# One core, post-norm decoder layer: the last batch's transposed self scores directly behind its self scores, and the work of the last steps placed anew

## The reference, cut to what matters

```
x = layernorm(x + self_attention(x))        # causal; rms norm and rope on q and k
x = layernorm(x + cross_attention(x, ctx))  # causal; q from x, k and v from ctx
x = layernorm(x + light_ffn(x) + heavy_ffn(x))
```

## Time and profile before

| what | value |
|---|---|
| median of three runs | 978.58 us (974.46 to 981.06) |
| the profiled execution, its own time | 978.16 us |
| its span, first to last instruction | 976.4 us |
| what lies around the span | 1.76 us |
| mean granted PE clock | 0.96 |
| busy, share of the span | PE 91%, PEld 71%, DVE 74%, ACT 51%, POOL 55% |
| DMA queue of SP | 50.5% of 16 engines |

### The profile page before, as it was taken

The page is one execution under the profiler, slowest core; times in us unless marked ns, Lnnn a source line. Parts: engine busy times, 40 slices in busy tenths (PEclk is TensorE's granted clock), DMA queues, the critical chain, the costliest instruction groups (busy, mean ns, idle before and its releaser), DMA issues. The chain is left out here.

```text
span 976.4 us, 21698 instructions
## 1 busy us (share of the span) xinstructions
PE 888.3 (91%) x7712; PEld 689.7 (71%) x7712; DVE 725.3 (74%) x1764; ACT 496.8 (51%) x1063; POOL 537.9 (55%) x1047
## 2 busy tenths in 40 slices
PE   3367897999999999999999999999999999999886
PEld 2335565787868787777878787877778686767576
DVE  7788687878788878879787888788887877663411
ACT  1132444646475655656464756556464746455332
POOL 7554465646564756656565647657565656162421
PEclk9669898999999999999999999999999999999888
DMA  3794383727476654818275666738283656613000
GB/s 110 120 173 68 52 110 50 106 33 109 51 100 78 98 78 65 111 37 110 34 119 59 100 78 80 97 54 107 44 109 42 95 72 88 77 31 49 14 11 21
DMA packets 79644, 74.22 MB, mean 76 GB/s; under 512 B 8593, under 2 KB 78897, under 8 KB 79537
## 3 DMA queue, kind: packets, MB, share of 16 engines
q1 hardware_dynamic: 75008, 68.11, 50.5%
q10 hardware_dynamic: 4528, 4.73, 1.9%
HBM read 17.49 MB, written 4.20 MB: 22 GB/s over the span
## 5 line engine op out<-in xcount | busy, mean ns | idle before, releaser
L768 ACT ACTIVATE pr<-bank 128x384 f32<-128x384 f32 x512 | 240.0, 500 | 188.1 <-PE bank L370 187.0
L946 DVE TENSOR_REDUCE mx<-bank 128x3 f32<-128x384 f32 x512 | 266.4, 552 | 89.7 <-PE bank L370 87.5
L1311 POOL TENSOR_SCALAR_AFFINE_SELECT pr<-pr 128x256 f32<-128x256 f32 x512 | 222.1, 448 | 132.3 <-ACT pr L768 130.1
L370 PE MATMUL bank<-w,g 128*128 128x256 f32 x576 | 170.8, 389 | 1.1 <-ACT g L780 1.1
L370 PE MATMUL bank<-cmaskb,idb 128*128 128x256 bf16 x512 | 143.3, 280 | 27.7 <-DMA stk2k<-nat1k 13.7
L780 ACT ACTIVATE g<-bank,b 128x256 f32<-128x256 f32 x144 | 67.8, 473 | 83.5 <-PE bank L370 83.2
L1335 POOL TENSOR_TENSOR xTlow<-xT,xThigh 128x512 fp32r<-128x512 f32 x16 | 20.8, 1301 | 149.8 <-ACT xThigh L702 149.8
L370 PEld LDWEIGHTS bank<-w,g 128*128 128x128 f32 x576 | 89.6, 190 | 5.2 <-ACT g L780 1.5
L370 PEld LDWEIGHTS bank<-cmaskb,idb 128*128 128x128 bf16 x512 | 50.1, 98 | 50.5 <-DVE mx L946 22.5
L370 PE MATMUL bank<-stk2k,stk2q 97*128 97x128 bf16 (+1 forms) x512 | 85.1, 253 | 0.0
L370 PE MATMUL bank<-stk1q,stk1k 100*128 100x256 bf16 (+1 forms) x512 | 80.1, 254 | 2.4 <-DMA stk1q<-mT 1.0
(11 more groups left out here) (166 smaller groups left out, 1832.5 us busy)
## 6 DMA issues: line engine op xcount, KB each, us to landing
stk1q<-nat1q SPq DMA_DIRECT2D x90, 128.0 KB, 4.5
stk1k<-nat1k SPq DMA_DIRECT2D x90, 128.0 KB, 5.4
stk2k<-nat2k SPq DMA_DIRECT2D x90, 128.0 KB, 4.6
stk2q<-nat2q SPq DMA_DIRECT2D x90, 128.0 KB, 5.7
xT<-in_xT SPq DMA_DIRECT2D x16, 256.0 KB, 5.9
ctxT<-in_ctxT SPq DMA_DIRECT2D x16, 256.0 KB, 6.0
x<-in_x SPq DMA_DIRECT2D x16, 256.0 KB, 5.7
out_x<-x SPq DMA_DIRECT2D x16, 256.0 KB, 2.2
```

The lines of the kernel that those rows point to most:

```text
L370: return nc.tensor.matmul(out, lhsT, rhs, start=start, stop=stop, skip_group_check=check)
L768: nc.scalar.activation(pr[:, h % (2 * HG), :], ring_bank("T", a, b, h)[:, 0:3 * P], ACT.Exp, scale=HD ** -0.5)\
L946: V.tensor_reduce(mx3[:, h, :], scored[:, 0:3 * P].rearrange("p (k t) -> p k t", k=3), AX.X, ALU.max, negate=True).then_inc(s_mx[a], 1)
L1311: G.affine_select(out=slot, in_=slot, compare_op=ALU.is_ge, fill=0.0, base=0, pattern=[[0, 2], [1, P]], channel_multiplier=-1).then_inc(s_ ...
```

## The change

Steps 15 and 16 get their own lists on PE (`last_self_step`, `last_cross_step`) and on DVE, and the order of turns of step 15 is S1(15), T1(15), S2(14), T2(14). The diff, cut:

```diff
+        turns = [turn for i in range(B + 1)
+                 for turn in ((("S", 1, i), ("T", 1, i), ("S", 2, i - 1), ("T", 2, i - 1)) if i == B - 1 else
+                              (("S", 1, i), ("S", 2, i - 1), ("T", 1, i), ("T", 2, i - 1)))
...
+            def last_self_step(s):
...
+                phase(lambda h: scores(1, s, h), others)
+                others = {}
+                for j in range(FCH):
+                    add(0, ffn_out, l, 0, j)
+                add(0, transpose_max, 1, s)
+                add(0, v2, c)
+                for j in range(FCH):
+                    add(0, ffn_out, l, 1, j)
+                add(LAST_K2_AT, k2, s)
+                for gr in range(NG - 1):
+                    add(HG * gr + VALUES_AFTER, values, 1, s, gr)
+                phase(lambda h: scores_t(1, s, h), others)
+                others = {}
+                add(LAST_OUT1_AT[0], values, 1, s, NG - 1)
+                add(LAST_OUT1_AT[1], out_proj, 1, s)
+                add(H, transpose_max, 2, c)
+                add(H, transpose_xn, f)
+                phase(lambda h: scores(2, c, h), others)
+                others = {}
+                add(LAST_Q2_AT[0], transpose_x1, s)
+                add(LAST_Q2_AT[1], q2, s)
+                for gr in range(NG - 1):
+                    add(HG * gr + VALUES_AFTER, values, 2, c, gr)
+                phase(lambda h: scores_t(2, c, h), others)
+            def last_cross_step(c):
...
+                add(0, values, 2, f, NG - 1)
+                add(TAIL_AT[0], out_tokens, f)
+                add(TAIL_AT[1], out_dims, f)
+                add(TAIL_AT[2], out_proj, 2, f)
+                add(TAIL_AT[3], v2, c)
+                for j in range(FCH):
+                    add(TAIL_HIDDEN_AT[j], hidden, l, j)
+                phase(lambda h: scores(2, c, h), others)
+                others = {}
+                for j in range(FCH):
+                    add(0, ffn_out, l, 0, j)
+                add(0, transpose_max, 2, c)
+                for j in range(FCH):
+                    add(0, ffn_out, l, 1, j)
+                add(LAST_XNT_AT, transpose_xn, f)
...
+                phase(lambda h: scores_t(2, c, h), others)
...
-                        add(HIDDEN_AT[j], hidden, l, j)
+                        add((TAIL_LAST_AT if f == B - 1 else HIDDEN_AT)[j], hidden, l, j)
...
-                    add(XNT_AT, transpose_xn, f)
+                    add(0 if f == B - 1 else XNT_AT, transpose_xn, f)
```

On ACT, copy_x1(15) and the parts of q2(15) move from the head of step 16 to the exponentials of T2(14), and the high part of k2(15) stands behind all of T1(15)'s exponentials:

```diff
+                if s == B - 1:
+                    copy_group(1, s, NG - 2)
+                    high_part(2, s, 1, 0)
+                    copy_group(1, s, NG - 1)
                 for h in range(H):
+                    if s == B - 1 and h == LAST_COPY_AT[0]:
+                        copy_x1(s)
+                        high_part(2, s, 0, 1)
+                    if B - 1 <= s <= B and h == LAST_COPY_AT[1]:
+                        copy_xn(f)
+                    if s == B - 1 and h == LAST_COPY_AT[2]:
+                        mid_part(2, s, 0, 1)
```

On DVE (step 15; step 16 has a like list), and the constants:

```diff
+                max_t(1, s)
+                statistics(2, f)
+                layer_norm(2, f)
+                scale2(f)
...
+                add_residual(3, l, FFN_BANK, x2b)
+                statistics(3, l)
+                take_rest(2, s, 1, 0)
+                split_rest(2, s, 1, 0)
+                divide_pair(s, 0)
...
+                maxima(2, c, {LAST_DVE_AT[0]: lambda: divide_pair(s, 1), LAST_DVE_AT[1]: self_residual,
+                              LAST_DVE_AT[2]: lambda: layer_norm(1, s)})
+                max_parts(2, c)
+                max_t(2, c)
+                take_rest(2, s, 0, 1)
+                low_xn(f)
+                low_part(2, s, 0, 1)
...
+LAST_K2_AT, LAST_OUT1_AT, LAST_Q2_AT, LAST_XNT_AT = 4, (2, 8), (1, 3), 6
+TAIL_AT = (3, 6, 9, 13)
+TAIL_HIDDEN_AT = (2, 2, 4, 5, 7, 8, 10, 11, 12)
+TAIL_LAST_AT = (6, 6, 11, 13, 13, 14, 14, 16, 16)
+COPY2_LAST, LAST_COPY_AT, LAST_DVE_AT, TAIL_DVE_AT = 2, (2, 3, 5), (3, 9, 12), (5, 12)
```

More of the change, by code:

```diff
@@ L222, in iterations @@
                 step(i)
-        turns = [turn for i in range(B + 1) for turn in (("S", 1, i), ("S", 2, i - 1), ("T", 1, i), ("T", 2, i - 1))
+        turns = [turn for i in range(B + 1)
+                 for turn in ((("S", 1, i), ("T", 1, i), ("S", 2, i - 1), ("T", 2, i - 1)) if i == B - 1 else
+                              (("S", 1, i), ("S", 2, i - 1), ("T", 1, i), ("T", 2, i - 1)))
                  if 0 <= turn[2] < B]
@@ L624, in phase, with add @@
                         heads(h)
+            def last_self_step(s):
+                c, f, l = s - 1, s - 2, s - 3
+                others = {}
+                def add(at, fn, *args):
+                    others.setdefault(at, []).append(lambda: fn(*args))
+                add(X1T_AT, transpose_x1, c)
+                add(OUT2_AT[0], values, 2, f, NG - 1)
+                add(Q2_AT, q2, c)
+                add(OUT2_AT[1], out_tokens, f)
+                add(OUT2_AT[2], out_dims, f)
+                add(OUT2_AT[3], out_proj, 2, f)
+                for j in range(FCH):
+                    add(HIDDEN_AT[j], hidden, l, j)
+                phase(lambda h: scores(1, s, h), others)
[22 more added lines that the diff above has]
+                phase(lambda h: scores_t(2, c, h), others)
@@ new lines, in last_cross_step, with add @@
+            def last_cross_step(c):
+                f, l = c - 1, c - 2
+                others = {}
+                def add(at, fn, *args):
+                    others.setdefault(at, []).append(lambda: fn(*args))
+                add(0, values, 2, f, NG - 1)
[6 more added lines that the diff above has]
+                phase(lambda h: scores(2, c, h), others)
+                others = {}
+                for j in range(FCH):
+                    add(0, ffn_out, l, 0, j)
+                add(0, transpose_max, 2, c)
+                for j in range(FCH):
+                    add(0, ffn_out, l, 1, j)
+                add(LAST_XNT_AT, transpose_xn, f)
+                for gr in range(NG - 1):
+                    add(HG * gr + VALUES_AFTER, values, 2, c, gr)
+                phase(lambda h: scores_t(2, c, h), others)
@@ L626, in step @@
             def step(i):
                 s, c, f, l = i, i - 1, i - 2, i - 3
+                if s == B - 1:
+                    return last_self_step(s)
+                if c == B - 1:
+                    return last_cross_step(c)
                 others = {}
@@ L797, in step @@
                     copy_group(2, f, NG - 2)
-                if live(c):
+                if live(c) and c < B - 1:
                     copy_x1(c)
@@ L801, in step @@
                     copy_group(2, f, NG - 1)
-                if live(c):
+                if live(c) and c < B - 1:
                     high_part(2, c, 0, 1)
                 for j in range(FCH):
-                    if j == COPY2_AT and live(f):
+                    if j == (COPY2_LAST if f == B - 1 else COPY2_AT) and live(f):
                         copy_out(f)
-                    if j == MIDQ_AT and live(c):
+                    if j == MIDQ_AT and live(c) and c < B - 1:
                         mid_part(2, c, 0, 1)
@@ L836, in step @@
                         exponential(1, s, h)
-                    if h == COPY_XN_AT and live(f):
+                    if h == COPY_XN_AT and live(f) and not B - 3 <= f < B - 1:
                         copy_xn(f)
+                if s == B - 1:
+                    copy_group(1, s, NG - 2)
+                    high_part(2, s, 1, 0)
+                    copy_group(1, s, NG - 1)
                 for h in range(H):
-                    if live(s):
+                    if s == B - 1 and h == LAST_COPY_AT[0]:
[5 more added lines that the diff above has]
+                        mid_part(2, s, 0, 1)
+                    if live(s) and s < B - 1:
                         if h == COPY1_AT[0]:
@@ L1113, in low_xn, with last_self_step, self_residual, last_cross_step @@
                                 xnh[:, :, :].bitcast(f32), ALU.subtract).then_inc(s_xnT, 1)
+            def last_self_step(s):
+                c, f, l = s - 1, s - 2, s - 3
+                maxima(1, s, {NORM2_AT: lambda: normalise_cross_heads(f), SPLITQ_AT: lambda: take_rest(2, c, 0, 1),
+                              LOWQ_AT: lambda: low_part(2, c, 0, 1)})
+                max_parts(1, s)
+                dve.wait_ge(s_x1c, f + 1)
+                add_residual(2, f, PROJ_BANK[2], x1c)
+                max_t(1, s)
+                statistics(2, f)
+                layer_norm(2, f)
+                scale2(f)
+                dve.wait_ge(s_x2b, l + 1)
+                add_residual(3, l, FFN_BANK, x2b)
[3 more added lines that the diff above has]
+                divide_pair(s, 0)
+                def self_residual():
+                    dve.wait_ge(s_x0, 16 * (s + 1))
+                    add_residual(1, s, PROJ_BANK[1], x0)
+                    statistics(1, s)
```

(28 more changed lines are left out.)

## The result

The changed kernel took 995.69 us (993.01 to 998.52, four runs), the kernel before 979.55 in as many (974.46 to 981.06): a ratio of 1.0174 (of the means), 95% interval 1.0126 to 1.0223, so 1.7% slower. Beside the later runs the kernel before was measured anew, with medians of 974.28 us (runs 1 to 4), 975.07 (5 to 8), 973.68 (9 and 10) and 974.59 (11), and their ratios are against these. Ratios of different runs, and the changed kernel's, therefore do not stand on one scale; against these four the changed kernel would be some 2.2% slower (an estimate, 995.69 over their mean, 974.4). The forecast was 989.6, in a range of 974 to 999. The profiled execution took 996.69 us, its span 994.2: 6.3 more than the 987.9 of the sum.

The account below looks back on a forecast made before the run. PE's work was taken as the time over most of the run, DVE as setting the pace in the changed S2(14). Stages followed along PE from 849.3 gave a span of 987.9; with 1.76 around it 989.6 us, range 974 to 999.

Parts of the forecast that it names:

- Step 1: Before T1(15): what is left of ffn_out(12), and v2(14), take 10.3 us on PE and hide the chain of maxima.
- Step 2: T1(15), with k2(15) and three groups of values, takes 10.2 us and ends at 869.8.
- Step 3: S2(14): DVE sets the pace, first maximum only at 875.0; out_proj(15) at 1.2 GHz adds 1.7; T2(14) starts at 894.7.
- Step 4: T2(14) with x1T(15) and q2(15): 14.4 us, of which 2.1 for x1T and q2 at 1.2 GHz; S2(15) at 909.1.
- 9.0 for a bare phase: In T2(14): the length of a phase standing alone, 9.0 us, taken from T1(1).
- The DMA taken as 0: Before S2(15): batch 15's key parts, queued on SP behind T2(14)'s maxima, could be 0 to 1.8 us late; taken as 0.
- Steps 5 and 6: S2(15) with hidden(13) and v2 beside it 17.6 us, then ffn_out(13) 8.0 and transpose_max 0.25, hiding T2(15)'s maxima.
- Steps 7 and 8: T2(15) to its last values, 9.0 and 0.9 us at full clock, then 21.2 to hidden(15) instead of 23.8.
- Step 9: From hidden(15) to the end: 21.9 us instead of 23.4, with 1.5 of clock loss given back.
- the clock is lost in each T phase: Rival: T1(15) takes 1.8 us more, T2(15) and its tokens 2.7 + 1.4; 995.5 us, chance 0.17.
- DVE keeps up: Rival: DVE reaches S2(14)'s first maximum in time, T2(14) starts 12 us earlier; 977.5 or 975.4 us, chance 0.15.
- The clock holds: Rival: PE stays at 2.4 GHz in S2(14), x1T and q2, so 1.7 and 2.1 fall away; 985.8 us, chance 0.20.

Follow-up runs that it names:

- run 1: The changed kernel with the rest and split of k2(15) on DVE moved from ahead of S2(14)'s maxima to behind them; 989.30 us, ratio 1.0153.
- run 2: The changed kernel with the second half of ffn_out(12) moved from ahead of T1(15) into S2(14), its residual behind max_t; 994.40 us, ratio 1.0208.
- run 3: The changed kernel with 124 unread constant products in PE's waits in T1(15), S2(14), T2(14) and T2(15); from hidden(12) on 140.3 us against 144.2.
- run 4: The kernel before with only the tail's placing changed (hidden(14) order, copy_out of batch 15, xnT(15)); 972.65 us, ratio 0.9985.
- run 5: The changed kernel with hidden(13) and the end of cross attention 14 ahead of S2(15) again, ffn_out(13) within S2(15); 997.92 us, ratio 1.0242.
- run 7: The changed kernel with half of ffn_out(12) in S2(14), transpose_max and v2(14) first in the gap, split of k2(15) behind S2(14)'s maxima; 988.67 us, ratio 1.0145.
- run 8: The kernel before with the tail placing of run 4 and 44 unread constant products in T2(14) and T2(15); 972.05 us, ratio 0.9970.
- run 9: The changed kernel with POOL's norm of batch 11 behind T1(15)'s masks and batch 13's second root between them; 994.83 us, ratio 1.0219.
- run 10: The kernel of run 7 with POOL's order of run 9 and unread constant products in T2(14) and T2(15); 987.50 us, ratio 1.0142.
- run 11: The kernel of run 7 with POOL's order of run 9 and no constant products; 987.29 us, ratio 1.0111.

## Why the prediction was right, and where its sum was short

The forecast's direction, mechanism and place were right; the sum was 5.6 us short from hidden(12) on (11.5 more than before, where the traces show 17.1), and the span began this part 0.7 later. The direction had some luck: slower stood at 0.50 and no change at 0.44, and a miss as large to the other side, 983.5, would have shown no change. Of the signs, PE's wait for DVE behind the third head and the wait for the maxima's DMA ahead of T2(14) came; T1(15) ended at 872.3 (870), T2(14) began at 896.7 (893 to 895), S2(15) at 914.0 (909), and T2(15) took 11.5 to its last values (under 10.5).

- *Step 1, the gap:* 10.5 against 10.3, the maxima hidden as forecast. What it missed stands on POOL: the gap holds v2(14) back, and with it the queue ahead of T1(15)'s masks.
- *Step 2, T1(15):* 11.8 against 10.2. The wait for POOL costs 1.2 (10.8 in run 5, 9.6 in run 9) and the lower clock 1.0 (11.8 against run 5's 10.8). The term "partly in a wait for masks" was too small.
- *Step 3, S2(14):* 24.4 against 24.9, right in its parts too: the first maximum 5.0 behind the first head (5.2 in the sum), out_proj at 1.2 GHz. Runs 1 and 2 show that DVE's queue, not PE's work, sets it.
- *Step 4, T2(14):* 17.4 against 14.4, the largest miss. The term "9.0 for a bare phase" ended at the last head, but the values of group 3 stand ahead of S2(15)'s first head: 1.06 of wait and 0.8 (the row at 913.17). With these 1.9 the sum is 16.3, near run 7's 16.4. ACT's wait for q2 came as in the sum, 3.87 us (1.9 and most of the 2.1 there). The other 1.0 is the clock, which stayed low through the first values (1.51). The DMA taken as 0 was hidden by that, and cost 1.02 in run 3, where it was not.
- *Steps 5 and 6:* 25.2 against 25.9.
- *Steps 7 and 8:* 33.0 against 31.1. The term "bare 9.0 and 0.9" is 10.6 at full clock (run 7), 0.7 more, and the clock took 0.9 (11.5 to the last values); hidden(15) came 21.5 behind them, not 21.2.
- *Step 9:* 22.0 against 21.9.

So of the rivals, "the clock is lost in each T phase" came true by half: T1(15) and T2(15) lost it for under a third of the phase, 1.0 and 0.9 us, not 1.8 and 4.1. The rule of the Trainium skill ("TensorE: Matmul & The Clock Gate", section "HAM oscillation — how this bites in real kernels") that bursts with waits between them can fall to the lower level agrees with the row at 868.04, the second group of values behind the wait of 2.10. Run 5, with the same wait of 2.12 in T1(15), kept 0.86 in all its values: there the measurement goes the other way. "DVE keeps up" was undone by the queue that the forecast named, and run 1, which takes the split out of it, gives 5.3 us and not the change back. "The clock holds" fell at out_proj and q2; where products hold it (run 3), 3.8 us come back.

Why the change is slower is settled as to its place, and in part as to its causes. Runs 4 and 5 put the loss into step 15. In the changed kernel's trace 13.0 us go up to S2(15) (63.9 from the end of hidden(12) to S2(15), 50.9 before; 8.9 in the forecast); behind that it takes 80.2 (76.2 before, 78.8 in the forecast). Of the 13.0, 5.3 are the split of k ahead of the maxima (1.5 of it out_proj's clock), 1.2 the order on POOL, and some 3 the clock in T1(15) and T2(14) (1.0 by run 5, 2.0 by run 3, of which S2(15) there gave 1.3 up again).

The rest is argued, from rows. An estimate from the best stage of each run (7.5 + 9.6 + 19.6 + 15.4 + 25.1 + 32.0 + 22.0 = 131.2) still lies 4.1 above the 127.1 of before, and 8.8 above the 122.4 of run 4, which has the same tail and so is the fair measure. What is left is the chain from T1(15) to T2(14) with less beside it: in run 7 PE is idle for 6.4 us of S2(14), where DVE works 16.3 of 19.6, and for 3.7 of T2(14), against 4.8 from 849.3 to 900.2 before. No run reached that sum, and whether hidden(13), placed in S2(14), would cover it was not tried.

## What to carry to other kernels

Before moving a phase, write down for each engine what stands in its queue ahead of the first instruction that the moved phase waits for; one split of k ahead of the first maximum cost 5.3 us here, and a norm moved out of the way on POOL came back as a wait on DVE. A phase's length, taken from another place of the trace, ends where the next phase can start, not at its own last product. And work put beside a dependent chain is worth only what the chain's slowest queue leaves: run 2 hid 4 us of products in S2(14) and the median fell by 1.3 us, since the first values behind the place it left were timed by POOL.

## What the runs showed of the hardware that was not expected

The clock in a phase with short waits is not a property of the code alone. The sixteen products of T2(15)'s first values, behind the same dense block, took 1.51 us in the changed kernel's profile and 0.86 in those of runs 1, 7 and 9; over the two T phases and what follows, the same instructions differed by 8.1 us between runs 7 and 11. That is more than most of the edits tried here were worth, and it fits the scatter of run 11 on one chip: its shortest execution, 983.74, had a mean granted clock of 0.965, its longest, 990.80, one of 0.946. That constant products narrow the spread is not shown: run 10, with them, spread over 1.9 us, run 7, without, over 1.5.

Constant products put into a wait can run at 1.2 GHz themselves: ten of them took 2.34 us in run 10 (row at 890.39) and 1.25 in run 8 at full clock (row at 912.45), so they are cheap only where the clock is still high.
